# An adaLN block of gated cumulative attention and routed experts: the order of the setup and of batch 0, and when the q,k product is signalled

## The reference, cut to what matters

```python
mod = silu(c) @ wmod                        # six vectors per batch: sa, ca, ga, sb, cb, gb
ga, gb = sign * max(|.|, 0.25)              # of ga and gb each
h = layernorm(x) * (1 + ca) + sa
q, k, v = split(rms_norm(h) @ w_qkv.T)      # q, k rms-normed again
w = exp(k);  kv = w * v
y = sigmoid(q) * cumsum(kv) / (cumsum(w) + 1e-6)     # sums over the tokens of a batch
u, g = split(y @ w_swiglu.T)
x = x + ga * (h + (u * silu(g)) @ w_out.T)
h = layernorm(x) * (1 + cb) + sb
# top-1 router over 16 experts, at most 320 tokens each, ranks by a cumulative sum over all tokens
x = x + gb * combine(gelu(dispatch(h) @ w1) @ w2)
```

## Time and profile before

| | us |
|---|---|
| median of 3 runs | 220.8 |
| lowest and highest | 220.46, 223.25 |
| the profiled execution | 221.19 |
| its span, first to last instruction | 219.4 |

### The profile page before, as it was taken

How to read it: one execution, slowest core, us unless ns; L and a number is a source line. 1 busy time by engine, 2 the same in 40 slices (tenths; PEclk the granted TensorE clock), 3 DMA queues, 4 the chain that set the end, 5 groups by cost and what they waited for, 6 DMA issues and landing times.

```text
span 219.4 us, 3971 instructions
## 1 busy us (share of the span) xinstructions
PE 189.2 (86%) x1155; PEld 153.1 (70%) x1155; DVE 152.5 (70%) x480; ACT 150.9 (69%) x438; POOL 101.8 (46%) x115
## 2 busy tenths in 40 slices
PE   7979989998998999698685688999999999999800
PEld 4858678687875888566474445887888988879700
DVE  3799799998999889999943407184766847576400
ACT  5398999999999999986535642585585864835000
POOL 6130132442046347556785550005575665767770
PEclk9999999999999999999975579999999999999975
DMA  4999999991104113412452217999969663310010
GB/s 137 307 343 358 359 344 321 341 276 56 51 0 142 57 48 114 150 72 76 172 179 94 78 39 192 363 356 357 335 207 348 213 186 101 137 37 28 24 37 0
DMA packets 37284, 38.60 MB, mean 176 GB/s; under 512 B 2591, under 2 KB 31334, under 8 KB 37264
## 3 DMA queue, kind: packets, MB, share of 16 engines
q1 hardware_dynamic: 33936, 31.29, 45.8%
q0 software_dynamic: 3328, 7.07, 9.0%
HBM read 19.19 MB, written 18.95 MB: 174 GB/s over the span
## 4 chain that ended last, share of the span: by engine, by line
PE 50%; DVE 15%; ACT 11%; issue 8%; POOL 6%; DMA 3%; SPq 1%; POOLq 1%; DVEq 0%; ACTq 0%
PE bank L1213 14%; PE bank L1199 11%; PE bank L981 5%; POOL out_dram L455 4%; ACT junk L491 3%; ACT ewkv L510 3%; PE bank L1033 2%; PE bank L1035 2%; DMA wmod<-in_L_wmod_dram 2%; POOL dispatched_rows L433 2%; DVE w1l L897 2%; PE bank L998 2%; PE bank L1170 2%; PE bank L1050 2%; PE bank L1019 2%
## 5 line engine op out<-in xcount | busy, mean ns | idle before, releaser
L455 POOL DMA_INDIRECT out_dram<-x_all,rest x40 | 42.5, 1062 | 40.7 <-DVE x_all L927 30.9
L433 POOL DMA_INDIRECT dispatched_rows<-rows,slot x32 | 31.5, 983 | 18.1 <-DVE slot L815 9.6
L652 ACT ACTIVATE HT<-bank 128x320 f32<-128x320 f32 x64 | 28.0, 438 | 10.2 <-PE bank L1199 9.8
L1213 PE MATMUL bank<-HT,w 128*128 128x320 f32 x112 | 32.4, 432 | 0.0
L1213 PEld LDWEIGHTS bank<-HT,w 128*128 128x128 f32 x112 | 20.6, 189 | 6.7
L1199 PE MATMUL bank<-xth,w1h 128*128 128x320 f32 x64 | 22.6, 354 | 0.2 <-DVE xtl L903 0.2
L897 DVE TENSOR_TENSOR w1l<-w,w1h 128x1024 fp32r<-128x1024 f32 x8 | 16.2, 2031 | 6.9 <-DMA dispatched_rows<-rows,slot 6.9
L946 DVE COPY OT<-bank 128x320 f32<-128x320 f32 x14 | 6.9, 492 | 18.5 <-PE bank L1213 18.5
L1199 PE MATMUL bank<-xth,w1l 128*128 128x320 f32 x64 | 19.8, 309 | 0.0
L1199 PE MATMUL bank<-xtl,w1h 128*128 128x320 f32 x64 | 19.8, 309 | 0.0
L491 ACT ACTIVATE junk<-bank 128x128 f32<-128x128 f32 x64 | 16.6, 290 | 2.6 <-PE bank L981 2.6
(11 more groups left out here) (163 smaller groups left out, 475.2 us busy)
## 6 DMA issues: line engine op xcount, KB each, us to landing
w<-in_L_ffn_w_dram SPq DMA_DIRECT2D x16, 512.0 KB, 8.1
dispatched_rows<-blank SPq DMA_DIRECT2D x8, 965.0 KB, 12.5
rest<-dispatched_rows SPq DMA_DIRECT2D x8, 645.0 KB, 6.0
hin<-dispatched_rows SPq DMA_DIRECT2D x7, 320.0 KB, 7.0
x_all<-in_L_attn_x_dram SPq DMA_DIRECT2D x8, 256.0 KB, 4.6
rows<-gb_row SPq DMA_DIRECT2D x8, 256.0 KB, 6.7
out_dram<-rows SPq DMA_DIRECT2D x8, 256.0 KB, 2.3
out_dram<-x_all,rest POOLq DMA_INDIRECT x40, 2.6
```

The costliest lines, as they stand in the source:

```text
L433: pool.indirect_dma_start(out=disp_d, out_offset=bass.IndirectOffsetOnAxis(ap=slot[:, b, j:j + 1], axis=0), in_=rows[:, b, j, :], in_offse ...
L455: pool.indirect_dma_start(out=out_d.rearrange("b t d -> (b t) d"), out_offset=bass.IndirectOffsetOnAxis(ap=rest[i % RING][:, n, C_TOK - D: ...
L652: act.activation(HT[e][:, f, :], ps_h[c % HB][:, 0:CAP], ACT.Gelu_apprx_tanh).then_inc(h_done, 1)
L1213: last = pe.matmul(ps_o[e], w2[i % RING][:, e, f, :], HT[e][:, f, :], start=(f == 0), stop=(f == NF - 1))
```

## The change

- `w_in` counts only the load of the q,k,v weights; the gate and swiglu weights count on a new semaphore `w_more`. The loads keep their order.
- PE transposes the q,k,v weights before the first modulation products, in place of one constant matmul, and signals them. The gate and swiglu weights are transposed after `transpose1(0)`, into ps_u, and ACT copies them out in the new `keep_more`, between `ln1_scale(1)` and `square_sums(0)`.
- `modulation_products` moves from behind `transpose1(0)` to behind `transpose1(1)`. On DVE `modulations()` moves behind `normalize1(1)`, `h_means(0)` and `qk_means(0)`, and `diagonal(0)` with it.
- Single constant matmuls stand behind `weights_over` and on both sides of `modulation_products`. They write ps_g.
- `project_qk` signals after each of its two banks, and `square_sums` waits for the first bank at block 0 and for the second at block 2.
- `exp_qk` takes the four k exponentials first and signals them with `ek_done`, for which `weigh_v` and `transpose_k` now wait; then the four q exponentials, which signal `ew_done` as before.

```diff
@@ sync
-            sp.dma_start(gw[:, :], gate_w_d).then_inc(w_in, 16)
-            sp.dma_start(wsw[:, :, :], w_swiglu_d.rearrange("(m e) d -> e m d", m=2)).then_inc(w_in, 16)
+            sp.dma_start(gw[:, :], gate_w_d).then_inc(w_more, 16)
+            sp.dma_start(wsw[:, :, :], w_swiglu_d.rearrange("(m e) d -> e m d", m=2)).then_inc(w_more, 16)
@@ scalar
             def square_sums(b):
-                after(act, qk_ps, b)
                 after(act, nrm_b, b, 1)
                 for j in range(NJ):
+                    if j % 2 == 0:
+                        after(act, qk_ps, 2 * b + j // 2)
@@
-                for j in range(NJ):
-                    for m in range(2):
+                for m, done in ((1, ek_done), (0, ew_done)):
+                    for j in range(NJ):
                         last = act.activation(t[:, j, m, :], ps_qk[:, j, m * D:(m + 1) * D], ACT.Exp,
                                               scale=nrr[:, 2 * j + m:2 * j + m + 1])
-                last.then_inc(ew_done, 1)
+                    last.then_inc(done, 1)
@@
-                act.copy(wqkvT[:, D:3 * D], bank01[:, D:3 * D])
-                act.copy(wswT[:, :], bank01[:, 512:512 + 2 * D])
-                act.copy(gwT[:, :], bank01[:, 512 + 2 * D:512 + 2 * D + NE]).then_inc(wt_done, 1)
+                act.copy(wqkvT[:, D:3 * D], bank01[:, D:3 * D]).then_inc(wt_done, 1)
+
+            def keep_more():
+                act.wait_ge(wt_ps, 2)
+                act.copy(wswT[:, :], ps_u[:, 0:2 * D])
+                act.copy(gwT[:, :], ps_u[:, 2 * D:2 * D + NE]).then_inc(wt_done, 1)
@@
-            ln1_scale(0); keep_weights(); modulate1(0); ln1_scale(1); square_sums(0); modulate1(1)
+            ln1_scale(0); keep_weights(); modulate1(0); ln1_scale(1); keep_more(); square_sums(0); modulate1(1)
@@ vector
             def weigh_v(b):
                 after(dve, v_ps, b)
-                after(dve, ew_done, b)
+                after(dve, ek_done, b)
@@
-            stats1(1); aggregate1(1); modulations(); normalize1(1); diagonal(0); h_means(0)
-            qk_means(0); diagonal(1); stats1(2); aggregate1(2); stats1(3); weigh_v(0); normalize1(2)
+            stats1(1); aggregate1(1); normalize1(1); h_means(0); qk_means(0); modulations()
+            diagonal(0); diagonal(1); stats1(2); aggregate1(2); stats1(3); weigh_v(0); normalize1(2)
@@ tensor
-                last.then_inc(qk_ps, 1)
+                    if j % 2 == 1:
+                        last.then_inc(qk_ps, 1)
@@
             def transpose_k(b):
-                after(pe, ew_done, b)
+                after(pe, ek_done, b)
@@ run_early
-                    pe.matmul(bank2[:, 0:256], tri[:, P:2 * P], tri[:, P:P + 256], start=True, stop=True)
+                    pe.matmul(ps_g[:, 0:256], tri[:, P:2 * P], tri[:, P:P + 256], start=True, stop=True)
@@
-            run_early(1)
+            pe.wait_ge(w_in, 16)
+            for m in range(3):
+                last = pe.transpose(bank01[:, m * D:(m + 1) * D], wqkv[:, m, :], ident[:, :])
+            last.then_inc(wt_ps, 1)
@@
             def weights_over():
-                pe.wait_ge(w_in, 48)
-                for m in range(3):
-                    pe.transpose(bank01[:, m * D:(m + 1) * D], wqkv[:, m, :], ident[:, :])
+                claim(pe, "u", wt_done, 1)
+                pe.wait_ge(w_more, 32)
                 for m in range(2):
-                    pe.transpose(bank01[:, 512 + m * D:512 + (m + 1) * D], wsw[:, m, :], ident[:, :])
-                pe.transpose(bank01[:, 512 + 2 * D:512 + 2 * D + NE], gw[:, :], ident[0:NE, 0:NE]
-                             ).then_inc(wt_ps, 1)
+                    pe.transpose(ps_u[:, m * D:(m + 1) * D], wsw[:, m, :], ident[:, :])
+                pe.transpose(ps_u[:, 2 * D:2 * D + NE], gw[:, :], ident[0:NE, 0:NE]).then_inc(wt_ps, 1)
@@
-            weights_over(); transpose1(0); modulation_products(); project_qk(0); h_square_sums(0)
-            transpose1(1); project_v(0); row_product(0); row_product(1); project_qk(1); transpose_k(0)
+            transpose1(0); weights_over(); run_early(1); project_qk(0); h_square_sums(0)
+            transpose1(1); run_early(1); modulation_products(); run_early(1); project_v(0); row_product(0); row_product(1); project_qk(1); transpose_k(0)
```

More of the change, by code:

```diff
@@ L206, in adaln_attention_moe @@
         c_in, wmod_in, w_in, blank_out = [sem(n) for n in ("c_in", "wmod_in", "w_in", "blank_out")]
-        wmod_rest, wout_in = sem("wmod_rest"), sem("wout_in")
+        wmod_rest, wout_in, w_more = sem("wmod_rest"), sem("wout_in"), sem("w_more")
         mod1_done = sem("mod1_done")
@@ L234, in adaln_attention_moe @@
         pool_past = sem("pool_past")
+        ek_done = sem("ek_done")
         last_sent = sem("last_sent")
```

## The result

| | before | changed |
|---|---|---|
| median, us | 222.03 (4 runs) | 224.39 (4 runs) |
| lowest to highest, us | 220.46 to 225.56 | 223.95 to 224.81 |
| profiled execution, span, us | 221.19, 219.4 | 224.81, 223.0 |

The changed kernel takes 1.0157 times as long, 95% interval 1.0106 to 1.0209: about 3.5 us of time, 3.6 us of span. The forecast was 1.0% slower. The same pair measured again on two chips gave 1.0096 [1.0028, 1.0165] and 1.0132 [1.0054, 1.0210]. Executions of most kernels here, the one before too, fall into a faster and a slower state some 2% apart; ratios are of executions in the faster state alone (as few as two of a kernel), medians of all of them.

The account below looks back on a forecast made before the run. Bound: PE, DVE and ACT, all full from 26 to 100 us. DVE's queue +2.8 and later batches -0.5 gave +2.3 us, so 223.1 us against the medians, 1.0% slower; range 219.5 to 226.0, 8 times in 10.

Parts of the forecast that it names:

- 1 us early up to the exponentials of batch 0: Opening: weights first and bank-by-bank signals start batch 0's exponentials at about 13.65 instead of 14.69 us.
- Modulations at 13.75, then 6.5 us of queue, weigh_v(0) at 20.2: Opening, DVE: late modulation products hold up its queue, so weigh_v(0) starts at 20.2 instead of 17.39, 2.8 us later.
- The earlier k is worth nothing here: Opening: k's exponentials ready at 14.7 instead of 16.9 us gain nothing, since weigh_v(0) waits its turn on DVE.
- PE enters no later than DVE: Start of the full stretch: only DVE's 2.8 us lag was counted, with PE standing at row_product(0) until 17.0.
- rival A: Opening: PE at half rate if its activity thins out, all 2.5 us later on top, 225.6 us; chance 15%.
- 0.6 us back from the later batches, less 0.1: Later batches, 26 to 100 us: k's exponentials first gain 0.6 of at most 1.0 us, less 0.1 for added waits.
- The lag is carried unchanged to the end: From 26 to 100 us: engines are nearly full, with 3.6 us (DVE) or 2.7 us (ACT) idle to catch up.
- rival C: From 26 to 100 us: the lag is worked off in slack or by earlier k, 220.8 us, no change; chance 13%.
- Rival B: End of stage, 108.6 to 122.4 us: a later clock fall shortens PE's chain up to 3.5 us, 219.6 us; chance 12%.

Follow-up runs that it names:

- the signals alone: The kernel before plus only bank-by-bank signals of the q,k product and k's exponentials first; 1.0024 [0.9910, 1.0138] times the kernel before.
- the modulations in idle time: Changed kernel with modulation products ahead of the q,k product and DVE's modulations between normalize1(1) and batch 0's means; second run 0.9964 [0.9909, 1.0019] of the kernel before.
- the early products with DVE's order as in the change: Changed kernel with modulation products ahead of the q,k product on PE, but DVE's modulations still behind batch 0's means; 1.0110 [0.9998, 1.0221] of the kernel before.
- only the new setup order: Changed kernel without bank-by-bank signals and without k's exponentials first; 1.0164 [1.0072, 1.0256] times the kernel before.

## Why the prediction was right, point by point

The sign, the place and the mechanism of the opening held; the sum was 2.3 us and the measured ratio makes it 3.5. The median of 224.39 us lies in the wide range and just above the forecast's own, 222 to 224.3. That the sum came this near is partly luck: the queue's lag was put 0.8 us too high and a gain of 0.5 us was subtracted that did not come, while PE's wait (0.65 us) and the later fall of the clock (1.2 us) were not in it.

- *1 us early up to the exponentials of batch 0.* Right, and undersized: 1.75 us. Batch 1's statistics started sooner, and `square_sums` began at 9.6, not at 10.3.
- *Modulations at 13.75, then 6.5 us of queue, weigh_v(0) at 20.2.* Three versions bear the mechanism out: the loss goes when the modulations go back, no difference from before is shown when they fill idle time, and 2.17 us of the queue can be moved in front of them. The modulations came at 13.01 and the queue took 6.38 us: 19.39, 2.0 us late instead of 2.8.
- *The earlier k is worth nothing here.* Right: weigh_v(0) waited for its turn.
- *PE enters no later than DVE.* This term was missing from the sum. The denominator lags 2.66 us where weigh_v lags 2.0: scan_w(0) waits 0.65 us for PE, whose row products ran at half rate behind the stop. I had this stop in rival A, as part of a slow start; it came alone, and in two of the three profiles of the changed kernel.
- *0.6 us back from the later batches, less 0.1.* Wrong. The lag is 2.6 us at batch 0 and 2.55 at batch 5, and the signals alone gain 0.05 us over five batches. The waits that the earlier trace rows counts were taken for a gain. Those before 72 us, 0.2 us for a transpose and 0.2 us for the q,k product, are gone from the changed kernel's profile, and the lag is hardly smaller. What held the engines instead was not followed.
- *The lag is carried unchanged to the end (rival C not).* Right up to 72 us, in full engines. Another 1.2 us fell between 72 and 90 us with a granted clock of 0.79. This is in all three profiles of the changed kernel, but also in one of the two of the kernel before. From batch 5's logarithm to batch 6's it is 16.35 to 16.58 us in the nine profiles of this document in which the clock falls there, and 15.11 to 15.71 us in the five in which it does not; among the nine is the second profile with the modulations in idle time, which has no late opening. So the 1.2 us go with the clock and not with the queue. How much more often the change meets the fall is open.
- *Rival B* (a faster end of the stage): not seen; the clock between 108.6 and 122.4 was 0.75 instead of 0.62 and POOL's last scatter began 3.6 us late (132.7 against 129.1).
- *Rival A* (half rate in the opening) happened in 5 of the 11 profiles of the changed kernel and its variants, and in one of two of the kernel before, where batch 0's logarithm is 3.2 us later for it. I took it for an effect of the change. No run shows that the change makes it more frequent, and it comes and goes with the same matmuls on one chip (last section). It may be part of why both kernels spread over several us; that is not shown.

## What to carry to other kernels

When setup work moves behind a batch's first steps, count everything that stands behind it in its engine's queue: here 6.4 us of work that needed none of that batch stood still with it, and idle time came where the engine had been full. Pull work that is ready into an engine's wait before shortening the chain that it waits for. Before counting a wait as a gain, ask what may hold the same engine next: here 0.4 us of such waits went and the lag shrank by 0.05 us.

## What the runs showed of the hardware

The time of PE's first full-rate matmul varies between executions of one program. The q,k product of the kernel before took 1.99 us from 9.30 in one profile and 3.45 us from 11.20 in another, on another chip. On one chip it varies too: the modulations in idle time and the early products with DVE's order as in the change have the same list of matmuls, and the product took 1.97 us from 9.22 in the first and 3.76 us from 11.29 in the second. The column of the granted clock reads 1.00 in all of these. The Trainium skill, "TensorE: Matmul & The Clock Gate", Part 1, says that the moment of release varies between runs, by about half a microsecond; the trace agrees that it varies, and shows more: full rate from about 6 us in one, from about 14 us in the other.

A short stop of PE does not decide whether the clock falls. Behind stops of 1.74 and 1.77 us the row products took 3.45 and 3.39 us; behind stops of 1.75 us (the changed kernel again) and 2.31 us (only the new setup order) they took 1.98 and 1.99 us.

DVE and POOL slow each other: the second diagonal takes 1.22 us alone and 2.06 us beside POOL's squaring, in the version with the modulations in idle time:

```profile
13.37 1.41 POOL L416 TENSOR_TENSOR hsq<-hT 128x512 f32<-128x512 f32 x1 [3.86 <-ACT hT L484]
```

POOL's own 1.04 us became 1.41 there. The Trainium skill, "GPSIMD Engine Reference", Architecture, has POOL's SBUF port shared with DVE, with which these two rows agree. Which of the two is the longer goes with which started first. In the kernel before, DVE's second diagonal starts first (14.09) and keeps its 1.22 us, and POOL's squaring takes 1.95; with only the new setup order POOL's squaring starts first and keeps its 1.04 us, and DVE's 8 columns take 1.03 instead of 0.16:

```profile
14.25 1.95 POOL L415 TENSOR_TENSOR hsq<-hT 128x512 f32<-128x512 f32 x1 [3.88 <-ACT hT L483]
13.56 1.04 POOL L416 TENSOR_TENSOR hsq<-hT 128x512 f32<-128x512 f32 x1 [3.88 <-ACT hT L484]
13.60 1.03 DVE L846 TENSOR_SCALAR mod<-mod_r 128x8 f32<-128x8 f32 x1
```
